# A transformer block on one core: the transposes, scaling and split of a tile's input at the very end of the slot before, in a new written-out order of all engines

## The reference

```
h = layernorm(x) * (1 + ca) + sa
q, k, v = rope(h @ Wq), rope(h @ Wk), h @ Wv             # 16 heads of 32
ck, cv  = weighted sums of k and v over blocks of 16     # 64 compressed blocks
out_comp = softmax(q ck, causal by block) @ cv
out_sel  = softmax(q k[pos], causal) @ v[pos]            # 16 positions, chosen by mean score of the blocks
out_win  = softmax(q k, the last 128 tokens) @ v
g = softmax(h @ Wg + bg)
x = x + ga * ((g0*out_comp + g1*out_sel + g2*out_win) @ Wo + bo)
h = layernorm(x) * (1 + cb) + sb
x = x + gb * (h @ base_W.T + base_b + shared LoRA(h) + the best 2 of 6 routed LoRAs(h))
```

## Time and profile before

| | |
|---|---|
| median of 2 runs | 2371.11 us (2369.42 to 2372.81) |
| the profiled execution's own time | 2375.0 us |
| its span in the profile | 2373.1 us |
| mean granted TensorE clock | 0.962 of full speed |
| PE busy | 2145.7 us, 90% |
| DVE busy | 1749.7 us, 74% |
| ACT busy | 1340.7 us, 56% |
| POOL busy | 788.2 us, 33% |
| DMA, mean rate | 38 GB/s |

### The profile page before, as it was taken

The page is one execution under the profiler, slowest core; times in us unless marked ns, Lnnn a source line. Parts: engine busy times, 40 slices in busy tenths (PEclk is TensorE's granted clock), DMA queues, the critical chain, the costliest instruction groups (busy, mean ns, idle before and its releaser), DMA issues.

```text
span 2373.1 us, 48974 instructions
## 1 busy us (share of the span) xinstructions
PE 2145.7 (90%) x17944; PEld 1427.3 (60%) x17944; DVE 1749.7 (74%) x4740; ACT 1340.7 (56%) x4701; POOL 788.2 (33%) x780
## 2 busy tenths in 40 slices
PE   4888999899998999989999899989999899997887
PEld 0665666566665666656665566656666566664454
DVE  3456888768886788768887688866887678875776
ACT  1244666556665566646656566655666556663664
POOL 0333333343333233333332433324333423333221
PEclk9998999999999999989999899999999999997989
DMA  6010000200011000110001100020001100011000
GB/s 233 19 40 15 23 28 24 68 22 28 28 32 63 28 24 28 46 49 19 28 28 41 54 28 24 23 76 24 22 25 45 50 28 28 24 46 45 19 19 19
DMA packets 48892, 89.64 MB, mean 38 GB/s; under 512 B 6760, under 2 KB 6760, under 8 KB 48656
## 3 DMA queue, kind: packets, MB, share of 16 engines
q1 hardware_dynamic: 39440, 69.74, 9.6%
q10 hardware_dynamic: 9216, 16.78, 1.9%
HBM read 69.68 MB, written 16.83 MB: 36 GB/s over the span
## 4 chain that ended last, share of the span: by engine, by line
PE 63%; DVE 22%; ACT 6%; issue 5%; POOL 2%; DMA 1%; SPq 0%; DVEq 0%; ACTq 0%; POOLq 0%
PE ps_m L702 9%; PE ps_o L634 7%; PE ps_m L506 6%; PE ps_m L667 5%; PE ps_m L507 5%; PE ps_m L508 5%; PE ps_s L628 4%; PE ps_t L610 4%; DVE ps_s L1548 4%; ACT pw L1033 3%; PE ps_m L684 3%; DVE wmax L1553 3%; PE ps_s L597 3%; PE ps_s L586 3%; PE ps_m L705 2%
## 5 line engine op out<-in xcount | busy, mean ns | idle before, releaser
L1033 ACT ACTIVATE pw<-ps_s,wmax 128x128 f32<-128x128 f32 x1024 | 360.3, 382 | 168.5 <-DVE wmax L1553 168.4
L506 PE MATMUL ps_m<-w_hi,h_hi 128*128 128x512 f32 x768 | 374.0, 487 | 35.1 <-DVE rbf L1520 18.9
L1043 ACT ACTIVATE pw<-pw,wden 128x128 f32<-128x128 f32 x1024 | 313.2, 401 | 5.0 <-DVE wden L1563 4.8
L507 PE MATMUL ps_m<-w_lo,h_hi 128*128 128x512 f32 x768 | 309.7, 403 | 0.0
L508 PE MATMUL ps_m<-w_hi,h_lo 128*128 128x512 f32 x768 | 308.5, 402 | 0.0
L1067 ACT ACTIVATE pT<-ps_s 80x512 f32<-80x512 f32 (+7 forms) x240 | 141.9, 591 | 255.6 <-PE ps_o L634 155.7
L1311 POOL TENSOR_TENSOR h_lo<-hT,h_hi 128x512 fp32r<-128x512 f32 x57 | 72.3, 1268 | 540.4 <-ACT h_hi L993 540.4
L702 PE MATMUL ps_m<-wbt_s,h2T 128*128 128x512 f32 x512 | 249.0, 604 | 0.0
L667 PE MATMUL ps_m<-wo_s,aT 128*128 128x512 f32 x512 | 247.8, 609 | 0.0
L1574 DVE COPY_PREDICATED pT<-keep_prev,ps_t 128x512 f32<-128x512 uint32 x224 | 164.3, 733 | 94.2 <-PE ps_t L610 90.2
L1033 ACT ACTIVATION_READ_ACCUMULATOR pw<-ps_s,wmax 128x1 f32 x1024 | 226.6, 221 | 0.0
(11 more groups left out here) (187 smaller groups left out, 4341.9 us busy)
## 6 DMA issues: line engine op xcount, KB each, us to landing
xa<-x_in SPq DMA_DIRECT2D x65, 256.0 KB, 3.0
xc<-x_in SPq DMA_DIRECT2D x64, 256.0 KB, 2.8
out<-t ACTq DMA_DIRECT2D x64, 256.0 KB, 2.0
wo_s<-wo_in SPq DMA_DIRECT2D x8, 1024.0 KB, 6.3
wbt_s<-wbt_in SPq DMA_DIRECT2D x8, 1024.0 KB
gbc<-gate_rows SPq DMA_DIRECT2D x24, 256.0 KB, 5.4
pw<-wmod_in SPq DMA_DIRECT2D x3, 1024.0 KB, 5.5
pT<-wmod_in SPq DMA_DIRECT2D x3, 1024.0 KB, 5.3
```

The lines of the kernel that those rows point to most:

```text
L506: pe_.matmul(ps[:], h_hi[:, c, :], w_hi[:, col, c, :], start=(c == 0), stop=False)
L507: pe_.matmul(ps[:], h_hi[:, c, :], w_lo[:, col, c, :], start=False, stop=False)
L1033: ins = act.activation(pw[:, hw, :], ps_w[:, j, i, 1, :], ACT.Exp, bias=wmax[:, hw:hw + 1], accum_out=wden[:, 0, hw:hw + 1])
L1043: act.activation(pw[:, hw, :], pw[:, hw, :], ACT.Copy, scale=wden[:, 2, hw:hw + 1]).then_inc(wn_ok, 1)
```

## The change

The unit "HT" of a tile, with its scaling and its split, is put at the end of the slot before: each of `first_slot`, `slot` and `turn` now closes with `transpose_h(seg, b, t + 1, Ta + 1)` on PE, with `h_scaled` and `split_h` of t + 1 on ACT, and with `split_h(Ta + 1)` on POOL (at the end of `turn`: `split_low(Ta + 1)` on DVE). ACT's `split_h` now also waits for Q, K and V of the present tile. The copy of the modulation rows of the next batch, which stood at the end of `turn` on DVE, is now `next_mod`, after the first `window_weights`. The last `turn` of the loop prepares a tile that nobody uses.

Around this the written-out orders and the bank tables are new in nearly every function, although what is computed is the same. The core of the diff:

```diff
+FIRST_ORDER = [("Q", 1), ("K", 0), ("Y", 1), ("G", 1), ("QT", 0), ("H2T", 0),
+               ("Z", 0), ("KT", 1), ("F", 0), ("ZT", 1), ("V", 1), ("HT", 1)]
-SLOT_ORDER = [("HT", 1), ("Y", 0), ("Q", 1), ("K", 1), ("QT", 0), ("G", 0),
-              ("H2T", 0), ("Z", 0), ("KT", 1), ("F", 0), ("ZT", 1), ("V", 1)]
+SLOT_ORDER = [("Y", 0), ("Q", 1), ("K", 1), ("QT", 0), ("G", 0), ("H2T", 0),
+              ("Z", 0), ("F", 0), ("KT", 1), ("ZT", 1), ("V", 1), ("HT", 1)]
+TURN_ORDER = [("Y", 0), ("Q", 1), ("K", 0), ("V", 1), ("QT", 0), ("KT", 0),
+              ("H2T", 0), ("Z", 0), ("G", 1), ("F", 0), ("ZT", 1), ("HT", 1)]
...
             def slot(seg, b, s):      # PE
                 cs_scores(b, s)
-                transpose_h(seg, b, t, Ta)
                 output(seg, b, t, [0])
...
                 project(seg, b, t, "V", 2, [3])
+                transpose_h(seg, b, t + 1, Ta + 1)
...
             def turn(seg, b):         # PE
                 if c2:
-                    output(seg, b, t, [0])
-                    transpose_h(seg, b, t, Ta)
+                    output(seg, b, t, [0, 1])
                 window_scores(ba, 0, 0)
...
+                    feed(seg, b, t, [3, NC])
+                transpose_h(seg, b, t + 1, Ta + 1)
...
             def slot(seg, b, s):      # ACT
-                h_scaled(seg, b, t, "HT", hT, mod_a, moda_ok, ba + 1)
-                split_h(seg, b, t, Ta)
                 window_exp(b, s, 0)
...
                 copy_v(seg, b, t)
+                h_scaled(seg, b, t + 1, "HT", hT, mod_a, moda_ok, ba + 1)
+                split_h(seg, b, t + 1, Ta + 1, t)
...
             def head(t):              # ACT
                 h_scaled(seg, b, t + 1, "HT", hT, mod_a, moda_ok, 1)
+                gate_exp(t)
+                split_h(seg, b, t + 1, t + 1, t)
                 copy_v(seg, b, t)
-                split_h(seg, b, t + 1, t + 1, t)
-                gate_exp(t)
...
             def turn(seg, b):         # POOL
                 weigh_keys(seg, b, t, Ta)
+                scale_out(ba)
                 deviation_a(Ta + 1)
                 cs_subtract(ba, 0)
-                scale_out(ba)
...
+            def next_mod(seg, b, ba):
+
+                dve.wait_ge(*m_done_at(seg, b, "HT", NT - 1))
+                mod_copy((ba + 1) % B, mod_a, 0, moda_ok)
...
             def slot(seg, b, s):      # DVE
                 window_weights(b, s, 0)
+                ln_scale(x1[:], mvc, vec, xc[:, t % 2, :], lnc, lncp, NT * b + t)
                 rope(seg, b, t, "Q")
                 window_max(b, s, 1)
                 cs_factor(b, s)
-                ln_scale(x1[:], mvc, vec, xc[:, t % 2, :], lnc, lncp, NT * b + t)
                 gates_soft(seg, b, t, Ta, 0)
                 split_probs(b, s, 0)
                 rope(seg, b, t, "K")
-                split_probs(b, s, 1)
                 window_weights(b, s, 1)
                 router(seg, b, t, 0)
+                split_probs(b, s, 1)
                 router(seg, b, t, 1)
...
             def turn(seg, b):         # DVE
                 cs_max(ba, 0)
                 if c2:
                     final(seg, b, t)
-                gates_soft(seg, b, t, Ta, 1)
-                mod_copy((ba + 1) % B, mod_a, 0, moda_ok)
+                split_low(Ta + 1)
```

More of the change, by code:

```diff
@@ L744, in first_slot @@
-                transpose_cs(b, 1, 2)
-                feed(seg, b, t, [2, 3])
-                transpose_window(b, 1, 2)
-                transpose_z(seg, b, t)
+                transpose_cs(b, 1, 1)
+                transpose_window(b, 1, 2)
+                feed(seg, b, t, [1])
+                transpose_z(seg, b, t)
+                feed(seg, b, t, [2])
+                project(seg, b, t, "V", 2, [0])
+                feed(seg, b, t, [3])
+                transpose_window(b, 1, 3)
+                cs_values(b, 1, 0)
@@ L904, in end_first @@
                 cs_values(b, 1, 3)
+                feed(seg, b, t, [NC])
             def end_slot(seg, b, s):
@@ L934, in end_slot @@
                 cs_values(b, s, 3)
-                feed(seg, b, t, [NC])
             def last(seg, b):
@@ L1738, in first_slot @@
                 window_max(b, 1, 0)
+                cs_factor(b, 0)
+                window_max(b, 1, 1)
                 window_weights(b, 1, 0)
-                split_low(Ta)
-                window_max(b, 1, 1)
-                cs_factor(b, 0)
                 rope(seg, b, t, "Q")
+                split_probs(b, 1, 0)
+                window_weights(b, 1, 1)
                 cs_mask(b, 1)
+                rope(seg, b, t, "K")
                 cs_max(b, 1)
-                rope(seg, b, t, "K")
-                split_probs(b, 1, 0)
                 residual(seg, b, t)
-                gates_soft(seg, b, t, Ta, 0)
                 ln_scale(x1[:], mvc, vec, xc[:, t % 2, :], lnc, lncp, NT * b + t)
                 cs_factor(b, 1)
+                gates_soft(seg, b, t, Ta, 0)
+                split_probs(b, 1, 1)
                 router(seg, b, t, 0)
-                window_weights(b, 1, 1)
-                sum_keys(Ta, t)
                 router(seg, b, t, 1)
-                split_probs(b, 1, 1)
+                split_probs(b, 1, 2)
                 ln_a(seg, b, t, Ta + 1, 1)
-                split_probs(b, 1, 2)
-                gates_soft(seg, b, t, Ta, 1)
                 split_probs(b, 1, 3)
                 final(seg, b, t)
+                gates_soft(seg, b, t, Ta, 1)
+                sum_keys(Ta, t)
                 sum_q(seg, b, t, Ta)
@@ L1799, in turn @@
                     residual(seg, b, t)
+                rope(seg, b, t, "Q")
                 window_weights(ba, 0, 0)
-                rope(seg, b, t, "Q")
+                next_mod(seg, b, ba)
                 window_max(ba, 0, 1)
+                split_probs(ba, 0, 0)
                 rope(seg, b, t, "K")
-                split_probs(ba, 0, 0)
                 sum_q(seg, b, t, Ta)
                 window_weights(ba, 0, 1)
+                split_probs(ba, 0, 1)
                 sum_queries(ba)
+                if c2:
+                    ln_scale(x1[:], mvc, vec, xc[:, t % 2, :], lnc, lncp, NT * b + t)
                 sum_keys(Ta, t)
                 finish_keys(ba)
-                if c2:
-                    ln_scale(x1[:], mvc, vec, xc[:, t % 2, :], lnc, lncp, NT * b + t)
-                split_probs(ba, 0, 1)
                 choose(ba)
+                split_probs(ba, 0, 2)
                 gather(seg, b, ba)
@@ L1816, in turn @@
                     router(seg, b, t, 0)
-                split_probs(ba, 0, 2)
+                split_probs(ba, 0, 3)
+                ln_a(seg, b + 1, t, Ta + 1, 0)
                 gates_soft(seg, b, t, Ta, 0)
```

245 lines of the change are left out of this document (121 added, 124 removed).

## The result

The changed kernel takes 2468.32 us (median of two runs, 2465.02 to 2471.61) against 2371.11. The ratio is 1.040, with a 95% interval of 1.037 to 1.044. The forecast was 1.6% slower; it came out 4.0% slower, above the range. The profiled execution has a span of 2463.2 us and a time of 2465.02.

The account below looks back on a forecast made before the run. PE was taken to set the pace over much of the span, DVE and ACT early in each slot. 2375.0 + 37 + 21 + 5 - 20 + 1 - 4 - 1 = 2414, median 3.9 lower: 2410 us, range 2368 to 2446.

Parts of the forecast that it names:

- The copy of V: End of first slots and slots: "HT" waits 0.75 us for ACT's copy of V, 49 times, +37 us (25 to 62).
- the transposes' part: Slots: transposes of tiles 1 to 6, 0.50 us each, leave PE's spare time, +21 us (0 to 21).
- the floor: Slots 5 to 7: DVE's small L1600 operation meets POOL, costing 0.9 in slot 5, giving 0.1 in 6 and 7; +5 us.
- the holes in the second half: Rival: in each slot's second half PE waits for a later DVE chain, 0.8 us a slot, 2444 us; chance 0.27.
- the early input: Rival: `h_lo` ready long before Q frees L1600, shortens first slots and partly hides transposes, 2347 us; chance 0.14.
- The heads: Prologue's heads: rounding no longer stands behind the copy of V, 0.6 us less each, -4 us.
- The turn: Turn: loses a 0.27 us wait for `h_lo`, gains about 0.4 for `pw`; +0.1 each, 1 us (-6 to +17).
- The end stages: Stages at the end: last feed chunk leaves their ends, an unused "HT" is added; -1 us (-6 to +5).
- 7 x -2.9 = -20 us (bounds -35 and +12): First slots without their ends: 2.9 us shorter each, from a second-layernorm wait shortened and a low-clock stretch saved.
- The slower start: First slot: the second window half comes 8.75 us from the stage's start instead of 6.97, slower by 1.8.
- If the clock then stays up: First slot: condition under which the low-clock stretch's extra 1.6 us are saved.
- A wait of about 0.9 instead of 2.14: First slot: PE's wait in us for the second layernorm before its transposes, which come at about 29.4 instead of 30.62.

Follow-up runs that it names:

- e6: Changed kernel with PSUM banks of every second slot and the turn mirrored, so "HT" goes to the bank F has left, not V's: 2426.1 us.
- e3: Changed kernel with the transposes of tiles 1 to 6 put back behind the next slot's `cs_scores` on PE: 2410.9 us.
- e13: Changed kernel with POOL's `residual_in` of slots 2 to 7 and the turn at the preceding slot's end, ahead of `split_h`: 2450.1 us.
- e7: The kernel before with only the changed order and PSUM banks of the prologue's heads: ratio 0.9994 to the kernel before.
- e1: Changed kernel with `cs_normalise` ahead of `residual_in` again in POOL's first slot: 2449.6 us.
- e2: Changed kernel with the next batch's first `xc` load issued ahead of the weight reloads and gate rows on SP: 2448.3 us.
- e8: e1 with 28 added matmuls, result thrown away, in each first slot's wait for exponentials: 2453.7 us.
- e10: e9 with 20 added matmuls, result thrown away, in the first slot's remaining wait for exponentials: 2441.6 us.
- e5: e1 with DVE's `window_max(b, 1, 0)` and the copy of `mod_c` ahead of `split_low` in the first slot: 2451.7 us.
- e9: e5 with e2's early load of the first `xc` tile as well: 2441.7 us.
- e14: e9 with 6 added matmuls, result thrown away, in PE's wait for the residual ahead of `gate_logits`: 2432.0 us.

## Why the prediction was wrong

**The slots were right.** Their share of the sum, with the turn and without the first slots' ends, was 55 us, and 62.7 were measured (66 with the turn's work that the table has in the first slot's column). The copy of V cost 0.84 us and not 0.75, which makes 4 (e6). L1600 met `residual_in` in slot 5 as said (1.07 us), and in slots 6 and 7 it was let go 0.4 us earlier than before (0.80 and 0.52 against 1.20 and 0.94), where the prediction had 0.3. But in three batches slot 5's clock was 0.95, 1 us each, which was in no term; the prediction named a clock under 1.00 in a slot as a sign against it. e3 shows the transposes' part and e13 that of the floor. L610's waits, the sign of the holes in the second half, did not come in the slots (33.5 to 33.65 us for slots 2 to 4), and the early input paid nothing.

**The heads gained less than the traced pair says.** The first `cs_scores` stands 3.6 us earlier in it, but e7, which has the new heads alone, starts it 2.3 us earlier (181.55), and the other runs with these heads start it at 179.3 to 183.8 us; the times can't confirm 4 us. **The turn** was forecast at +0.1 us each and took about 1.0 more, mostly by the wait of 1.28 us for `pw` that the sum had at 0.4: 7 us instead of 1, within its bounds of -6 and +17. No run took the turn's order back. The end stages were forecast at -1 and came out at +2.3: the first of them takes 29.04 against 25.43 us to its `cs_scores`, of which 1.1 are the last turn's own tail (feed chunk 1 and the unused "HT"), and the later ones but one are shorter. That was not tried.

**The failed step is the first slot, "7 x -2.9 = -20 us (bounds -35 and +12)".** With its end the sum held -12 us, and +28.6 were measured, 40 us more (38 with the stage's own ends). The slower start was there as said: 8.7 us from the first window half to the second, a wait of 7.53. Six of the seven first slots took 52.6 to 54.3 us, and the prediction had named one above 50 as a sign against it. What I left out or got wrong:

- POOL's `residual_in` was moved to the head of the slot, ahead of `cs_normalise`, and I did not follow what it waits for on the SP queue. It is 19 to 20 us (e1, e2). That row of the order stood in the difference, and the load's place behind the feed weights in the code. The kernel before showed no such wait, because the operation stood later there.
- "If the clock then stays up" was the wrong end of that condition. It stood at 0.50 behind the first wait as before. But e8 and e10, which hold it up there, gain nothing in all: the later stretches take it back, the second part at a clock of 0.89. That POOL's scaling of the weights and DVE's chain from Q's rope to the second layernorm come next is read from the rows of e5, and only POOL's part was tried (e9).
- "A wait of about 0.9 instead of 2.14" for the second layernorm became up to three waits, one of them for Y's bank, in which "G" now stands. Behind them the clock falls (0.88 in e9), in e14 only in part of the batches.

The other 20 us stay with the last two together. Each shows in its place, and e5, e9 and e14 on top of e1 take 18 of them back (2449.6 to 2432.0 us), with edits that the kernel before didn't have either; how the two share the sum is open. The bounds were too narrow for the reason that they came from DVE's and PE's rows alone.
